# A graph network with experts: the experts' second layer computed with features as rows and turned back

## The reference, cut to what matters

```python
def _L1_ffn_ref(x, Wr, br, W1, b1, W2, b2):          # E = 8 experts, H = F = 512
    logits = xt @ Wr + br
    probs = jax.nn.softmax(logits, axis=-1)
    G = jnp.max(probs, axis=-1)
    idx = jnp.argmax(probs, axis=-1)
    h1 = jax.nn.relu(jnp.einsum('nh,ehf->nef', xt, W1) + b1)
    eo = jnp.einsum('nef,efh->neh', h1, W2) + b2
    Eout = jnp.take_along_axis(eo, idx[:, None, None], axis=1)[:, 0, :]
    y = G[:, None] * Eout
...
x = x + _L1_ffn_ref(_layernorm(x, axis=-1)[None], ...)[0]
```

## Time and profile before

| | us |
|---|---|
| median of 3 runs | 525.3 (524.03 to 525.36) |
| the profiled execution | 522.8 |
| its span, first to last instruction | 521.0 |
| TensorE busy, share of the span | 484.3 (93%) |
| VectorE | 423.4 (81%) |
| ScalarE | 323.1 (62%) |
| GpSimd | 77.1 (15%) |

### The profile page before, as it was taken

One profiled execution on the slowest core, in us unless ns is written; L12 is line 12 of the kernel. 1 busy time (PEld: TensorE's weight loads), 2 busy tenths in 40 slices (PEclk: granted clock), 3 DMA queues, 4 the chain that ended last, 5 costly groups with the idle time before them and its releaser, 6 DMA issues.

```text
span 521.0 us, 11336 instructions
## 1 busy us (share of the span) xinstructions
PE 484.3 (93%) x4348; PEld 355.4 (68%) x4349; DVE 423.4 (81%) x862; ACT 323.1 (62%) x618; POOL 77.1 (15%) x96
## 2 busy tenths in 40 slices
PE   8989999993999999999999899898899999999995
PEld 4867777762899999997887545444465586777662
DVE  7788988898999999876888778985866676987961
ACT  6466666677899999972766823445322358876720
POOL 4100000000000000001121200223233420213222
PEclk9699999997899999999999899999999999999999
DMA  8970000003011111002000285000001139974111
GB/s 206 315 282 1 1 2 1 3 1 106 22 61 57 61 56 56 4 7 77 2 1 1 78 311 198 1 0 2 4 21 63 62 99 338 390 267 174 59 58 55
DMA packets 25538, 45.62 MB, mean 88 GB/s; under 512 B 6993, under 2 KB 7029, under 8 KB 25484
## 3 DMA queue, kind: packets, MB, share of 16 engines
q1 hardware_dynamic: 23500, 39.69, 22.0%
q0 software_dynamic: 1952, 5.18, 2.7%
q10 hardware_dynamic: 32, 0.01, 0.0%
HBM read 33.76 MB, written 11.95 MB: 88 GB/s over the span
## 4 chain that ended last, share of the span: by engine, by line
PE 48%; DVE 12%; issue 6%; POOL 3%; ACT 3%; DMA 1%; POOLq 0%; DVEq 0%
PE sums L1758 14%; PE sums L1991 8%; PE sums L1562 7%; PE sums L1962 6%; PE sums L1771 5%; POOL row L542 2%; DVE work L1193 2%; PE sums L1540 1%; DVE st L927 1%; POOL xperm_scratch L534 1%; PE sums L1948 1%; PE sums L1748 1%; ACT rings L584 1%; PE sums L1987 1%; DVE big L1356 1%
## 5 line engine op out<-in xcount | busy, mean ns | idle before, releaser
L1758 PE MATMUL sums<-big,work 128*128 128x130 f16 x1080 | 66.6, 224 | 8.6 <-DVE work L1193 8.6
L1758 PEld LDWEIGHTS sums<-big,work 128*128 128x128 f16 x1080 | 63.9, 100 | 10.1 <-issue 6.2
L1032 DVE TENSOR_TENSOR big<-mid 128x1024 f16<-128x1024 f16 (+1 forms) x88 | 59.5, 733 | 2.1 <-PE sums L1659 2.0
L1652 PE MATMUL sums<-big 128*128 128x180 f16 x320 | 57.6, 265 | 0.6 <-DVE big L1032 0.6
L1771 PE MATMUL sums<-big,mid 128*128 128x260 f16 x400 | 47.0, 275 | 0.1
L1859 PE MATMUL sums<-mid 128*128 128x512 f16 x200 | 46.4, 379 | 0.0
L1595 PE MATMUL sums<-big,rings 128*128 128x512 f16 x120 | 45.2, 377 | 0.4 <-issue 0.2
L605 ACT ACTIVATE mid<-sums 128x180 f32 x80 | 26.6, 332 | 29.3 <-PE sums L1659 28.6
L1771 PEld LDWEIGHTS sums<-big,mid 128*128 128x128 f16 x400 | 38.2, 96 | 7.5 <-issue 0.3
L703 ACT ACTIVATE aux<-aux,small 128x1250 f16<-128x1250 f32 x32 | 40.9, 1326 | 2.5 <-DVE work L1193 1.7
L703 ACT ACTIVATE mid<-aux,small 128x1250 f16<-128x1250 f32 x32 | 40.8, 1323 | 2.4 <-DVE work L1193 2.4
(11 more groups left out here) (327 smaller groups left out, 1067.3 us busy)
## 6 DMA issues: line engine op xcount, KB each, us to landing
big<-in_L_ffn_W SPq DMA_DIRECT2D x10, 1024.0 KB, 9.9
mid<-in_L_ffn_W SPq DMA_DIRECT2D x6, 1024.0 KB, 15.5
xperm_scratch<-work SPq DMA_DIRECT2D x1, 5753.0 KB, 19.0
aux<-thr_scratch SPq DMA_DIRECT2D x8, 640.0 KB, 3.8
aux<-xperm_scratch SPq DMA_DIRECT2D x9, 523.0 KB, 3.6
row<-in_x SPq DMA_DIRECT2D x1, 1280.0 KB
aux<-in_L_gnn_Ws SPq DMA_DIRECT2D x4, 256.0 KB, 4.4
row<-in_x SPq DMA_DIRECT2D x1, 1024.0 KB, 6.6
```

What stands on the lines that cost most here:

```text
L1032: return V.tensor_tensor(out.rearrange("p c (v two) -> p c v two", two=2), values.rearrange("p (v two) -> p v two", two=2).unsqueeze(1).to ...
L1652: mm(count_bank(base, k)[:, 0:RW], L_ring[:, slot, k * CH + j, :], R_ring[:, slot, k * CH + j, :], start=j == 0, stop=False)
L1758: ins = mm(acc_region(h, t), weighted[i // 2 % NC][:, s % 2, t * P:(t + 1) * P], VP[:, s, part, h, :, :].rearrange("p b f -> p (b f)"), st ...
```

## The change: what it does

- `m2` now has the form of `m1`: weights stationary, 208 tokens moving, 48 products per expert, in banks 4 and 5. Expert 0 has its own version (`m2_first`), which starts with half of the hidden features.
- A new function of ScalarE, `y_out`, takes a bank to SBUF as fp32, divides by 256 and adds b2 as a bias per partition: four instructions per expert. It writes where `be_bc` and `gb_bc` were.
- A new function of TensorE, `back_T`, turns these back: eight transposes in fp32 per expert, into banks 6 and 7. `result` then waits for them and has one small instruction less.
- b2 is loaded once as 32 rows of 128, turned by TensorE after the ranks and copied by VectorE. `pick16`, the zeroing, the cast and the split of b2 go.
- The three loops are ordered anew. TensorE: half of `m1(e + 1)`, `back_T(e - 1)`, the other half, `token_T(e + 2)`, `m2(e)`. `result(e - 1)` is now in round e, and `rows` and `gates` of an expert come a round later on ScalarE.

```diff
-        b2_nat = gb_bc[0:64, :]
-        b2_16 = be_bc[0:64, 0:D // 2].bitcast(F16)
+        y32 = [r[:, 0:2 * S1].rearrange("p (b m) -> p b m", b=2) for r in (be_bc, gb_bc)]
+        b2_nat = gb_bc[0:E1 * K, 0:P]
+        b2T = be_bc[:, 2 * S1:2 * S1 + E1 * K]
...
-            sp.wait_ge(sem("b2_zeroed"), 1)
-            for q in (0, 32):
-                sp.dma_start(b2_nat[q:q + E1, :], b2_d).then_inc(sem("ld_b2"), 16)
+            sp.wait_ge(sem("gb_free"), 1)
+            sp.dma_start(b2_nat, b2_d.rearrange("e (k p) -> (e k) p", p=P)).then_inc(sem("ld_b2"), 16)
...
-            nc.gpsimd.memset(all16, 1.0)
-            nc.gpsimd.memset(b2_nat, 0.0).then_inc(sem("b2_zeroed"), 1)
+            nc.gpsimd.memset(all16, 1.0).then_inc(sem("gb_free"), 1)
...
-            a.wait_ge(sem("ff_used"), T)
-            a.wait_ge(sem("ld_b2"), 32)
-            act(b2_16, b2_nat, ACT.Copy, scale=WS).then_inc(sem("b2_hi"), 1)
...
+            def hidden(e, q):
+                i = 2 * e + q
+                a.wait_ge(sem("m1_done"), i + 1)
+                if i >= 2:
+                    a.wait_ge(sem("h_lo16"), i - 1)
+                for b in range(2):
+                    f = 2 * q + b
+                    act(h32[:, q, b, :], bank[2 + q][:, b * S1:(b + 1) * S1], ACT.Relu,
+                        bias=b1T[:, e, f:f + 1], scale=1.0 / WS).then_inc(sem("h32_made"), 1)
+
+            def y_out(e):
+
+                if e >= 1:
+                    a.wait_ge(sem("out_psum"), 2 * e)
                 for q in range(2):
-                    i = 2 * e + q
-                    a.wait_ge(sem("m1_done"), i + 1)
-                    if i >= 2:
-                        a.wait_ge(sem("h_lo16"), i - 1)
+                    a.wait_ge(sem("m2_done"), 2 * e + q + 1)
                     for b in range(2):
-                        f = 2 * q + b
-                        act(h32[:, q, b, :], bank[2 + q][:, b * S1:(b + 1) * S1], ACT.Relu,
-                            bias=b1T[:, e, f:f + 1], scale=1.0 / WS).then_inc(sem("h32_made"), 1)
+                        f = e * K + 2 * q + b
+                        act(y32[q][:, b, :], bank[4 + q][:, b * S1:(b + 1) * S1], ACT.Identity,
+                            bias=b2T[:, f:f + 1], scale=1.0 / WS).then_inc(sem("y_made"), 1)
 
             x_hi(0)
             w_hi(1, 0)
-            hidden(0)
+            hidden(0, 0)
+            hidden(0, 1)
             rows(1)
             w_hi(2, 0)
             x_hi(1)
@@ -878,23 +883,26 @@
             w_hi(1, 1)
             x_hi(2)
             for e in range(E1):
+                if e >= 1:
+                    y_out(e - 1)
+                if e >= 2 and e + 2 < E1:
+                    rows(e + 2)
+                    gates(e + 2)
+                if e + 1 < E1:
+                    hidden(e + 1, 0)
                 if e >= 1 and e + 2 < E1:
                     x_hi(e + 2)
                 if e + 1 < E1:
-                    hidden(e + 1)
+                    hidden(e + 1, 1)
                 if e == 0:
                     rows(3)
-                    w_hi(3, 0)
                     for i in range(1, 4):
                         gates(i)
-                elif e + 3 < E1:
-                    if e == 1:
-                        w_hi(2, 1)
+                elif e + 1 < E1:
+                    w_hi(e + 1, 1)
+                if e + 3 < E1:
                     w_hi(e + 3, 0)
-                    rows(e + 3)
-                    gates(e + 3)
-                if e >= 1 and e + 2 < E1:
-                    w_hi(e + 2, 1)
+            y_out(E1 - 1)
...
-            V.tensor_tensor(pick16[:, :], ident16[0:64, 0:E1], ident16[0:64, 32:32 + E1], ALU.add)
-            v.wait_ge(sem("b2_hi"), 1)
-            V.scalar_tensor_tensor(b2_16[32:64, :], b2_nat[32:64, :], WS, b2_16[32:64, :], ALU.mult, ALU.subtract).then_inc(sem("b2_lo"), 1)
...
+            v.wait_ge(sem("b2_psum"), 1)
+            V.tensor_copy(b2T, bank[1][:, 0:E1 * K])
...
-                link(V.tensor_scalar(gate[:, r, :], gsum[:, r, :], WS, None, ALU.mult))
-                link(V.reciprocal(gate_ws[:, r, :], gate[:, r, :]))
+                link(V.reciprocal(gate[:, r, :], gsum[:, r, :]))
                 for j, m in enumerate((P, S1 - P)):
-                    v.wait_ge(sem("m2_done"), 2 * e + j + 1)
-                    V.scalar_tensor_tensor(xs[0:m, r, j, 0:D], bank[4 + 2 * (e % 2) + j][0:m, :], gate_ws[0:m, r, j:j + 1],
+                    v.wait_ge(sem("out_psum"), 2 * e + j + 1)
+                    V.scalar_tensor_tensor(xs[0:m, r, j, 0:D], bank[6 + j][0:m, :], gate[0:m, r, j:j + 1],
                                            xs[0:m, r, j, 0:D], ALU.mult, ALU.add).then_inc(sem("res_made"), 1)
 
             h_split(0)
             x_lo(1)
             split_w(2, 0)
-            result(0)
             x_lo(2)
             split_w(1, 1)
             for e in range(E1):
+                if e >= 1:
+                    result(e - 1)
                 if e >= 1 and e + 2 < E1:
                     x_lo(e + 2)
                 if e + 1 < E1:
                     h_split(e + 1)
-                if e == 1:
-                    split_w(2, 1)
+                if e >= 1 and e + 1 < E1:
+                    split_w(e + 1, 1)
                 if e + 3 < E1:
                     split_w(e + 3, 0)
-                if e >= 1:
-                    result(e)
-                    if e + 2 < E1:
-                        split_w(e + 2, 1)
+            result(E1 - 1)
...
+            pe.wait_ge(sem("ld_b2"), 16)
+            nc.tensor.transpose(bank[1][:, 0:E1 * K], b2_nat, ident[0:E1 * K, 0:E1 * K]).then_inc(sem("b2_psum"), 1)
...
-            def m2(e, blocks=(0, 1)):
+            def m2(e, halves=(0, 1)):
                 pe.wait_ge(sem("w_lo1"), e + 1)
-                if e >= 2:
-                    pe.wait_ge(sem("res_made"), 2 * (e - 1))
-                for j in blocks:
-                    m = (P, S1 - P)[j]
-                    mm(bank[4 + 2 * (e % 2) + j][0:m, :], pick16[:, e:e + 1].to_broadcast([64, m]), b2_16, start=True, stop=False)
-                    for n, (k, (wp, hp_)) in enumerate((k, c) for k in range(K) for c in PARTS):
-                        if n % (K // 2 * len(PARTS)) == 0:
-                            pe.wait_ge(sem("h_lo16"), 2 * e + k // 2 + 1)
-                        ins = mm(bank[4 + 2 * (e % 2) + j][0:m, :], hT16[:, e % 2, hp_, k, j * P:j * P + m],
-                                 W16[e % 2][1][:, wp, k, :], start=False, stop=n == 3 * K - 1)
+                for q in halves:
+                    pe.wait_ge(sem("y_made"), 4 * (e - 1) + 2 * q + 2)
+                    for b in range(2):
+                        f = slice((2 * q + b) * P, (2 * q + b + 1) * P)
+                        for n, (k, (wp, hp_)) in enumerate((k, c) for k in range(K) for c in PARTS):
+                            if q == 0 and b == 0 and n % (K // 2 * len(PARTS)) == 0:
+                                pe.wait_ge(sem("h_lo16"), 2 * e + k // 2 + 1)
+                            ins = mm(bank[4 + q][:, b * S1:(b + 1) * S1], W16[e % 2][1][:, wp, k, f],
+                                     hT16[:, e % 2, hp_, k, :], start=n == 0, stop=n == 3 * K - 1)
                     ins.then_inc(sem("m2_done"), 1)
 
+            def m2_first(hq):
+
+                pe.wait_ge(sem("w_lo1"), 1)
+                if hq == 0:
+                    for q in range(2):
+                        mm(bank[4 + q][:, 0:2 * S1], zero16[:, 0:P], zero16[:, :], start=True, stop=False)
+                pe.wait_ge(sem("h_lo16"), hq + 1)
+                for f in range(K):
+                    for k in (2 * hq, 2 * hq + 1):
+                        for n, (wp, hp_) in enumerate(PARTS):
+                            ins = mm(bank[4 + f // 2][:, f % 2 * S1:(f % 2 + 1) * S1], W16[0][1][:, wp, k, f * P:(f + 1) * P],
+                                     hT16[:, 0, hp_, k, :], start=False, stop=k == K - 1 and f % 2 == 1 and n == 2)
+                    if hq and f % 2:
+                        ins.then_inc(sem("m2_done"), 1)
+
+            def back_T(e):
+
+                pe.wait_ge(sem("y_made"), 4 * e + 4)
+                for j, m in enumerate((P, S1 - P)):
+                    if e >= 1:
+                        pe.wait_ge(sem("res_made"), 2 * (e - 1) + j + 1)
+                    for f in range(K):
+                        ins = nc.tensor.transpose(bank[6 + j][0:m, f * P:(f + 1) * P],
+                                                  y32[f // 2][:, f % 2, j * P:j * P + m], ident[:, :])
+                    ins.then_inc(sem("out_psum"), 1)
+
             m1_first()
-            pe.wait_ge(sem("b2_lo"), 1)
-            m2(0, (0,))
+            m2_first(0)
             pe.wait_ge(sem("te_ready"), 1)
             token_T(1)
-            m2(0, (1,))
+            m2_first(1)
             token_T(2)
             m1(1)
-            for e in range(1, E1):
-                if e + 1 < E1:
-                    m1(e + 1)
+            for e in range(1, E1 - 1):
```

(9 more changed lines are left out.)

7 lines of the change are left out of this document (2 added, 5 removed).

## The result

| | before | changed |
|---|---|---|
| median, us (22 executions each) | 524.54 | 528.58 |
| lowest to highest | 521.09 to 528.17 | 523.01 to 531.21 |
| span of the profiled execution | 521.0 | 524.4 |
| mean granted clock in it | 0.975 | 0.974 |

The changed kernel takes 1.0058 times as long, 95% interval 1.0035 to 1.008: slower, by some 3 us (1.8 to 4.2; the medians lie 4.0 apart). The forecast was 528.8. Profiles are of one execution each, and the profiled one of the changed kernel took 526.17 us.

What follows compares the result with a forecast made beforehand. TensorE was taken as the bound. Idle 4.5, rounds -3.3 and -0.8, end +1.6 give +2.0; early part -0.7 and clock +2.2 make +3.5 us, so 528.8 us from the 525.3 median, range 524.8 to 531.6.

Steps and rivals of the forecast that it cites:

- The round: Steady expert round on TensorE: 10.27 us instead of 11.10, winning 3.3 us in four rounds.
- The hole: TensorE idle 4.5 us before the first transposes back, waiting for expert 0's outputs queued on ScalarE; bounds 4.3 and 4.9.
- The clock: TensorE's granted clock falls in the 4.5 us idle gap and stays at half afterwards: 2.2 us lost, bounds 0 and 5.
- The end: Last rounds, late weights and serial finish, net of what their products save: 1.6 us more.
- The wait for the weights: TensorE waits 0.8 us before expert 7's second layer, as its second weights are cast late.
- the serial end: After the last products, outputs, transposes back and additions run one after another; last scatter at 519.3 against 517.34.
- The early part: Before the experts, removed bias instructions on VectorE and ScalarE gain 0.72 us; bounds 0 and 1.87.
- the 0.8 wait: TensorE's 0.8 us wait for GpSimd's addition stays, as VectorE's split holds that addition.
- the new transpose of the biases: With its copy, some 0.1 us where ScalarE's tokens set the time; priced at nothing.
- The clock stays up: Rival, 25%: TensorE's clock does not fall in the idle gap; +1.3 us, 526.6 us.
- Token loads become the bound: Rival, 15%: later results delay token rows, costing 0.8 us in each of four experts, some 3 us on top; 531.8 us.
- The hole is half as long: Rival, 10%: expert 0's outputs come some 2.3 us sooner and the clock holds; 523.2 us.

Runs made afterwards that it cites:

- experiment 1: Changed kernel with expert 0's four outputs moved ahead of expert 3's rows, the exponentials and the weight cast on ScalarE; median 528.61 us, ratio 1.0055 to the kernel before.
- Experiments 4: Changed kernel with VectorE's second weight split of expert 0 moved behind the fifth tile of the second graph layer; one execution, 526.57 us.
- 6: Changed kernel, order kept, with a fifth slot for token rows; one execution, 528.11 us.
- experiment 2: Changed kernel with 24 unused products of zeros on TensorE ahead of the first transposes back; 527.51 us, ratio 1.0064 to the kernel before.
- experiment 3: Changed kernel with expert 0's outputs first on ScalarE and its result ahead of the weight split on VectorE; 526.27 us, ratio 1.0021 to the kernel before.
- experiment 5: Changed kernel with expert 0's outputs and result earlier, gates in their own round, expert 7's second weight cast earlier, last transposes halved; one execution, 523.98 us.
- the reordered kernel with five slots: Changed kernel with outputs, result, gates, late weight cast and last transposes reordered, plus a fifth token-row slot; ratio 0.9909 to the kernel before.
- 8: Reordered five-slot kernel with VectorE's second weight split of expert 0 cut in four pieces behind tiles 3 to 6; 519.87 us, ratio 0.9924 to the kernel before.
- the control: The kernel before, with only a fifth token-row slot added; ratio 0.9992 to the kernel before.

## Why the prediction was right

**The round: right.** 10.27 was worked out; 10.22, 10.21, 10.29 and 10.39 were measured, four rounds -3.33 against -3.3. The way back takes 0.92 for eight transposes, 0.04 over the value taken, and the token transposes 0.74, 0.09 under it. The two rounds over 10.22 hold stalls of 0.1 and 0.2 us, of the token transposes in one and of the transposes back in the other.

**The hole: right.** 4.5 us with bounds 4.3 and 4.9; measured 4.33. ScalarE's order made it, as experiment 1 shows: with the outputs first it is gone. Four outputs take 1.37 us, close to the hidden layer's 1.40.

**The clock: right in kind, wrong in size.** This is the term that was mis-sized. The fall came 3.7 us into the gap, where 3.6 had been read off the end of the old trace. But the price was 1.33 rather than 2.2 us. The working took the one earlier gap as the measure of recovery, and read it a little short: a window from 133 to 134 with 0.68 puts the rise at 133.6, not 133.4, so 4.7 us at half clock and 2.4 lost. Experiments 4 and 6 had the same gap at 1.44 and 2.93. 2.2 lies within that, so the term should have been given as a range with no preferred value.

**The end: right, 0.28 short.** From expert 7's first layer on, 1.6 more than before was worked out, and 1.88 measured. The wait for the weights was 0.70 (0.8 forecast), and the serial end took from 516.28, ScalarE's last outputs, to 520.68.

**The early part: right mechanism, smaller gain.** VectorE's statistics for the tile came 0.70 us earlier (forecast 0.72), GpSimd's addition was held until 1.12 after the split, the 0.8 wait stayed, and ScalarE's 0.3 wait went. But VectorE's kept 0.2 of 0.3, and 0.47 us arrived at the first expert product. The other 0.23 is the new transpose of the biases, a term that the prediction put at nothing: from the start of the 16 transposes just ahead of it (L1906, now L1909) to that of the 16 products behind it 2.17 us pass, where it was 1.93.

**Sum.** Stretch: forecast +2.0 and 2.2 for the clock, 4.2; measured 3.52. Early part: forecast -0.7, measured -0.47. So the two parts that the change touches cost some 3.0 us where 3.5 had been forecast, and the misses are of opposite sign. That the span grew by 3.4, nearly the forecast, is in part luck: 0.35 of it had arisen before the second graph layer. So is the closeness of 528.8 to 528.58: the forecast started from a median of three executions, 525.3, where 22 give 524.54.

**The rivals.** "The clock stays up" is refuted by the windows, and its effect alone is measured by experiment 2: 1.33 us in the stage, given back to the token chain. "Token loads become the bound" did not hold in the changed kernel, but the margin was as thin as the working said: 1.2 us for expert 5's rows (1.0 forecast) and none for expert 6's, for which ScalarE waited 1.57 us.

```profile
483.59 1.52 ACT L833 ACTIVATE rings<-aux 128x512 f32<-128x512 f32 x2 [1.57 <-DMA aux<-xperm_scratch]
```

It cost TensorE time in each of experiments 1, 2, 3 and 5, where the hole or the slow clock behind it no longer covered it. The prediction priced this chain only for a TensorE that the hole had held back; what the chain allows without the hole it did not ask. "The hole is half as long" is refuted.

## What to carry to other kernels

A cheaper inner round is worth its saving only if every chain that closes once per round still closes in time. List these chains (here: the copy and cast circle on ScalarE, and result, scatter, load, rows) with their lengths beside the new round, before pricing the round. A length that holds a transfer is not fixed: look at what else is under way then, as a result that is ready sooner may only wait longer. When a new result must go back through an engine that works in order, look at the first time it is wanted: the steady round had 0.33 us to spare and the first one was 4.3 us short. And if removing a stall moves the time little, leave it removed and look for the second bound; two edits that were each worth next to nothing were worth 1.4% together.

## What the runs showed of the hardware

- **GpSimd beside VectorE.** The same f32 addition of 128x512 took 1.08 to 1.26 us alone, 1.68 and 3.12 us when it started 0.55 and 2.0 us before the end of a VectorE instruction pair with two SBUF inputs. It ended 1.12 to 1.13 us after them both times.
- **The same gap, three prices.** A gap of 4.33 us was followed by half clock until 2.8 us after work went on in the changed kernel, one of 4.33 until 3.0 us after in experiment 4, one of 4.34 until 6.0 us after in experiment 6. They cost 1.33, 1.44 and 2.93 us. The fall came 3.6 to 3.9 us after the last product.
- **The clock can fall without such a gap.** In the profile of the reordered kernel with five slots it fell at 420.2, when TensorE had waited nowhere longer than 0.34 us since 412, and stayed down until 430.4. From the zero products that end the aggregation to the first expert product it then took 15.27 us, where the changed kernel took 11.06 with the same instructions. It fell in that place in four of the twelve profiled executions: here, in experiments 2 and 8 and in the control, whose program is that of the kernel before there and took 14.16 us instead of 10.83. In these four TensorE had no wait over 0.94 us from 412 on. The cause is open; it is one source of the spread between executions.

```profile
418.00:420.00 2.00, 1.96 (x16) 1.64 (x14) 1.72 (x12) 0.69 (x2) 0.00 (x0) 1.00 0.72 249
420.00:422.00 2.00, 1.78 (x10) 1.46 (x9) 1.75 (x10) 1.61 (x3) 0.79 (x1) 0.55 0.03 8
...
428.00:430.00 2.00, 2.00 (x7) 1.94 (x7) 0.00 (x0) 0.00 (x0) 1.60 (x2) 0.50 0.37 134
430.00:432.00 2.00, 1.90 (x12) 1.40 (x11) 0.80 (x2) 1.27 (x3) 0.00 (x0) 0.89 0.33 103
```

- **Scatter to reload.** From the end of VectorE's additions through scatter and load to the start of ScalarE's rows, four experts on, with ScalarE waiting for the load: from expert 2 to expert 6 it took 8.7 us before, 8.8 in the changed kernel, 10.5, 11.3 and 12.1 in experiments 2, 3 and 5. For the other experts it was 7.6 to 8.1 before and in the changed kernel. What grew is the time until the scatter had landed, behind 2 MB of weights; it is read under experiment 3.
